# A three-part decoder layer on one core: w2 copied in DRAM and split in place, no weight pieces on GpSimd, sixteen tile buffers, two scatters in flight

## What is computed

```python
shared = _swiglu(flat @ w_in.T) @ w_out.T
g_probs = jax.nn.softmax(flat @ wg.T + gb, axis=-1)          # 2 groups
g_idx = jnp.argmax(g_probs, axis=-1)
e_logits = flat @ we.T + eb                                   # 8 experts, 4 in a group
masked = jnp.where(g_idx[:, None] == egid[None, :], e_logits, -jnp.inf)
p_expert = jax.nn.softmax(masked, axis=-1) * g_prob
topv, topi = jax.lax.top_k(p_expert, TOP_K)                   # TOP_K = 2
h = _swiglu(flat @ w1.T)                                      # 512 wide, the same for all experts
for e in range(NUM_EXPERTS):
    routed = routed + h * w_se[:, e:e + 1] @ w2[e].T
return (shared + routed).reshape(Bs, Ts, C)
```

## Time and profile before

| | us |
|---|---|
| timed runs, median of 3 (lowest, highest) | 945.33 (943.61, 945.38) |
| the profiled execution's own time | 941.11 |
| its span, first to last instruction | 939.3 |
| block 2 begins | about 649 |
| slot numbers known | 725.4 |
| scatters issued, first to last | 726.3 to 773.1 |
| first transposes of the expert loop | 790.4 |
| last PE work of the loop, gathers begin | about 870 to 873 |

### The profile page before, as it was taken

One profiled execution on the slowest core, in us unless ns is written; L12 is line 12 of the kernel. 1 busy time (PEld: TensorE's weight loads), 2 busy tenths in 40 slices (PEclk: granted clock), 3 DMA queues, 4 the chain that ended last, 5 costly groups with the idle time before them and its releaser, 6 DMA issues. The chain is left out here.

```text
span 939.3 us, 17987 instructions
## 1 busy us (share of the span) xinstructions
PE 851.3 (91%) x6115; PEld 741.0 (79%) x6115; DVE 596.2 (63%) x1513; ACT 546.3 (58%) x1667; POOL 304.0 (32%) x318
## 2 busy tenths in 40 slices
PE   8999999999999989999999999998787748999841
PEld 6788888888888878988988898896575637999731
DVE  5787787687778767667767766775768214333153
ACT  4877677677668776866677686775343113554110
POOL 1443124124123434421432341351333750000544
PEclk9999999999999999999999999999897969999976
DMA  7680000000001020000000020010120532664233
GB/s 240 245 312 2 1 0 0 0 0 0 0 1 46 24 68 1 1 23 1 0 22 0 0 80 9 1 46 1 67 68 23 206 152 95 205 199 149 79 90 112
DMA packets 34105, 60.35 MB, mean 64 GB/s; under 512 B 3460, under 2 KB 15108, under 8 KB 34052
## 3 DMA queue, kind: packets, MB, share of 16 engines
q1 hardware_dynamic: 29956, 47.07, 15.0%
q0 software_dynamic: 4096, 12.59, 4.0%
HBM read 33.83 MB, written 25.82 MB: 64 GB/s over the span
## 5 line engine op out<-in xcount | busy, mean ns | idle before, releaser
L420 POOL TENSOR_TENSOR prob<-prob,rsum 128x512 f32<-128x512 f32 x128 | 133.4, 1042 | 395.0 <-DVE rsum L613 395.0
L498 ACT ACTIVATE prob<-psS,nmin 128x128 f32<-128x128 f32 x512 | 181.4, 378 | 6.2 <-DVE nmin L597 3.6
L481 ACT ACTIVATE pT_hi<-psT 128x512 fp32r<-128x512 f32 x128 | 69.6, 595 | 85.6 <-PE psT L752 85.6
L498 ACT ACTIVATION_READ_ACCUMULATOR prob<-psS,nmin 128x1 f32 x512 | 111.9, 218 | 0.0
L582 DVE TENSOR_TENSOR oT_lo<-psT,oT_hi 64x512 fp32r<-64x512 f32 x128 | 88.1, 688 | 23.1 <-ACT oT_hi L486 21.1
L576 DVE TENSOR_TENSOR pT_lo<-psT,pT_hi 128x512 fp32r<-128x512 f32 x128 | 82.3, 685 | 1.6 <-ACT pT_hi L481 1.4
L486 ACT ACTIVATE oT_hi<-psT 64x512 fp32r<-64x512 f32 x128 | 76.1, 594 | 5.6 <-PE psT L143 3.9
L476 ACT ACTIVATE v_hi<-psW 128x512 fp32r<-128x512 f32 x64 | 38.3, 598 | 68.0 <-PE psW L143 68.0
L141 PE MATMUL psT<-pT_lo,v_hi 128*128 128x256 f32 x256 | 73.1, 285 | 4.6 <-DVE pT_lo L576 4.6
L570 DVE TENSOR_TENSOR v_lo<-psW,v_hi 128x512 fp32r<-128x512 f32 x64 | 44.2, 691 | 50.3 <-ACT v_hi L476 50.3
L1022 POOL DMA_INDIRECT stage<-ys,slot x32 | 32.6, 1017 | 128.1 <-DMA ys<-z 99.7
(11 more groups left out here) (252 smaller groups left out, 2501.4 us busy)
## 6 DMA issues: line engine op xcount, KB each, us to landing
hs<-zero SPq DMA_DIRECT2D x1, 9984.0 KB, 31.2
stage<-hs SPq DMA_DIRECT2D x39, 256.0 KB, 2.9
stage<-w SPq DMA_DIRECT2D x10, 512.0 KB, 3.4
ys<-z SPq DMA_DIRECT2D x39, 128.0 KB, 1.9
stage<-ctxT SPq DMA_DIRECT2D x4, 512.0 KB, 4.0
out<-xres SPq DMA_DIRECT2D x16, 128.0 KB
xres<-x SPq DMA_DIRECT2D x3, 512.0 KB, 7.6
stage<-wq SPq DMA_DIRECT2D x2, 512.0 KB, 3.9
```

Source lines behind the costliest of these rows:

```text
L420: nc.gpsimd.tensor_tensor(prob[:, r, :], prob[:, r, :], rsum[:, r].unsqueeze(2).broadcast_to([P, TPG, P]), ALU.mult).then_inc(prob_done, 1)
L481: nc.scalar.activation(pT[0][:, i, :], psT[:, i, :], ACT.Copy).then_inc(pT_hi, 1)
L498: e = nc.scalar.activation(prob[:, n, :], flat(psS[:])[:, n * P:(n + 1) * P], ACT.Exp, bias=nmin[:, n:n + 1], scale=-1.0, accum_out=psums[ ...
```

## The change

- w2 is copied in DRAM, early in block 1, into an internal tensor `w2_raw`. At the start of block 2, SyncE loads it in four DMAs of 1 MB straight into the tensor that later holds the low parts. ScalarE writes the high parts from there (`w2_hi_part`, eight pieces), and VectorE subtracts in place (`w2_lo_part`, eight pieces).
- w_in's parts are made at the end of block 1, the high part on ScalarE, the low part on VectorE, both between the last `pT_split` and the last `oT_split`. GpSimd makes no low part in block 2. The table for Silu is loaded before the last `pT_split`.
- Tiles 12 to 15 of h have slots of their own: `z` for 12 and 13, the routing's scratch tensors `above` and `ties` for 14 and 15 (these wait for `weights_known`).
- Each scatter of tile T for choice c waits until that of tile T-1 for the same choice has landed. The semaphores are per choice now.
- The routing ranks each expert among the 4 of its group instead of among 8, which halves the arrays; `unsel` and `wse` are written once after both rounds (`unselected`). Some units stand in another order to the routing on VectorE.

```diff
+        w2_raw = nc.dram_tensor("w2_raw", [HT, P, NE * D], F32, kind="Internal").ap()
...
-        H_AT = (6, 7, 10, 11, 2, 3, 4, 5, 8, 9, 0, 1)
+        H_AT = (6, 7, 8, 9, 10, 11, 0, 1, 2, 3, 4, 5)
...
+            pieces += [(k_rows(win), wq_hi[:], wq_lo[:], 1.0)]
...
                 sp.dma_start(hs.rearrange("(t p) d -> p t d", p=P),
                              zero[:].unsqueeze(1).broadcast_to([P, NT, HID])).then_inc(slots_zero, 16)
+                sp.dma_start(w2_raw, w2.rearrange("(k p) n -> k p n", p=P)).then_inc(w2_copied, 16)
                 sp.dma_start(craw, ctx_v[:, :, 0:GT]).then_inc(ctx_in, 16)
...
+                act.preload_act_table(ACT.Silu)
                 pT_split(STEPS)
+                act.wait_ge(qk_mm, 2 * STEPS)
+                weights_hi(act, N_ATT + 2, wq_hi[:])
                 oT_split(STEPS, 1)
...
                 pT_split(STEPS)
+                weights_lo(dve, N_ATT + 2, wq_lo[:], wq_hi[:])
                 oT_split(STEPS, 1)
...
+            def h_slot(T):
+
+                if T < HSLOTS:
+                    return chunk(H_AT[T])
+                if T < HSLOTS + 2:
+                    return flat(z[:, 2 * (T - HSLOTS):2 * (T - HSLOTS) + 2, :])
+                return (above, ties)[T - HSLOTS - 2][:]
...
-                for i in range(STAGES, len(late)):
-                    wait_lo(sp, LATE[i - STAGES])
-                    sp.dma_start(piece(N0 + i, late[i][0].shape), late[i][0]).then_inc(stage_in[(N0 + i) % STAGES], 16)
-
-                for n in range(REUSED):
-                    sp.wait_ge(scattered[n], 2 * CHOICES * 16)
-                sp.wait_ge(scattered_rest, (HSLOTS - REUSED) * CHOICES * 16)
+                sp.wait_ge(w2_copied, 16)
+                for k in range(HT):
+                    sp.dma_start(w2s[1][:, k, :].bitcast(F32), w2_raw[k]).then_inc(w2_in[k], 16)
+
+                for c in range(CHOICES):
+                    sp.wait_ge(scattered[c], B * 16)
...
                     for c in range(CHOICES):
+                        if T:
+                            pool.wait_ge(scattered[c], 16 * T)
                         d = nc.gpsimd.indirect_dma_start(
                             hs[:, :], bass.IndirectOffsetOnAxis(ap=slot[:, c, T:T + 1], axis=0), h_slot(T), None,
                             bounds_check=SLOTS - 1, oob_is_err=False)
-                        d.then_inc(scattered[T % HSLOTS] if T % HSLOTS < REUSED else scattered_rest, 16)
+                        d.then_inc(scattered[c], 16)
...
+                def w2_hi_part(i):
+                    k, c = W2_PARTS[i]
+                    act.wait_ge(w2_in[k], 16)
+                    nc.scalar.activation(w2s[0][:, k, c], w2s[1][:, k, c].bitcast(F32), ACT.Copy).then_inc(w2_hi, 1)
...
+                def w2_lo_part(i):
+                    k, c = W2_PARTS[i]
+                    dve.wait_ge(w2_hi, i + 1)
+                    nc.vector.tensor_tensor(w2s[1][:, k, c], w2s[1][:, k, c].bitcast(F32), w2s[0][:, k, c].bitcast(F32),
+                                            ALU.subtract).then_inc(w2_lo, 1)
...
-                for u in range(14, UNITS.index("S10") + 1):
+                for u in range(14, UNITS.index("S10")):
                     unit(u)
+                    w2_lo_part(u - 14)
+                w2_lo_part(6)
+                unit(UNITS.index("S10"))
+                w2_lo_part(7)
```

More of the change, by code:

```diff
@@ L242, in build @@
                    ("xk", "upper"), ("xr", "upper"), ("w1", "lower"), ("w1", "upper"))]
-        PIECES += ["win", "wout"] + [f"w2 {k} {half}" for k in range(HT) for half in ("lower", "upper")]
+        PIECES += ["win", "wout"]
         BY_POOL = ("wk upper", "wr lower", "wr upper", "xv upper", "xr lower", "xk upper", "xr upper",
-                   "w1 lower", "win", "w2 0 lower", "w2 0 upper", "w2 1 lower", "w2 1 upper", "w2 2 lower", "w2 2 upper",
-                   "w2 3 lower")
+                   "w1 lower")
         def wait_lo(eng, name):
@@ L394, in _ @@
                     load(sp, n, pieces[n][0])
-                for i in range(STAGES):
-                    load(sp, len(pieces) + i, late_sources[i])
+                load(sp, len(pieces), late_sources[0])
                 sp.wait_ge(slots_zero, 16)
@@ L928, in build @@
             GSTEPS = 19
[L929 to L934 removed]
+            N0 = PIECES.index("wout")
+            late = [(late_sources[0], wouts[0][:], wouts[1][:])]
+            W2_PARTS = [(k, slice(c * INNER, (c + 1) * INNER)) for k in range(HT) for c in range(2)]
             ROUND = (range(0, 3 * TPG), range(3 * TPG, B))
@@ L1082, in _ @@
                 unit(8)
-                late_hi(4)
-                late_hi(5)
+                bias(3)
                 exps(0)
-                bias(3)
+                w2_hi_part(1)
                 unit(9)
-                late_hi(6)
-                late_hi(7)
+                w2_hi_part(2)
                 exps(1)
                 unit(10)
-                late_hi(8)
-                late_hi(9)
-                for u in range(11, UNITS.index("S10") + 1):
+                w2_hi_part(3)
+                unit(11)
+                w2_hi_part(4)
+                unit(12)
+                w2_hi_part(5)
+                unit(13)
+                w2_hi_part(6)
+                unit(14)
+                w2_hi_part(7)
+                for u in range(15, UNITS.index("S10") + 1):
                     unit(u)
@@ L1164, in gate_ranks @@
                     n = len(ROUND[r])
-                    pe_ = probs[:, tiles, GROUPS:NG]
-                    gsum_, esum_, chosen_, coef_ = (t[:, tiles] for t in (gsum, esum, chosen, coef))
-                    above_, ties_ = above[:, 0:n], ties[:, 0:n]
+                    gsum_, esum_, chosen_, coef_, picked_ = (t[:, tiles] for t in (gsum, esum, chosen, coef, picked))
+                    above_, ties_ = (t[:, 0:n * GROUPS * PER_GROUP * PER_GROUP].rearrange(
+                        "p (t a b) -> p t a b", a=PER_GROUP, b=PER_GROUP) for t in (above, ties))
+                    rank4 = rank[:, tiles].rearrange("p t (g e) -> p (t g) e", g=GROUPS)
                     link, linked = chain(gate_step, r * GSTEPS + 4)
@@ L1312, in _ @@
                 split("S03")
-                unit(8)
                 dve.wait_ge(gate_copied, 3)
@@ L1316, in _ @@
                 gate_maxima(0)
+                unit(8)
                 gate_ranks(0)
@@ L1491, in _ @@
                 pe.wait_ge(experts_known, 1)
[L1492 to L1493 removed]
+                pe.wait_ge(w2_lo, len(W2_PARTS))
                 turn(0)
```

108 lines of the change are left out of this document (41 added, 67 removed).

## The result

The changed kernel takes 917.51 us (median of four runs, 917.14 to 917.67) against 945.36 for the kernel before (four runs, 943.61 to 945.77): a ratio of 0.971, 95% interval 0.969 to 0.973. The forecast was 927.0 with a range of 914 to 938. The time lies in the range; the gain is 27.8 us where 18.3 were forecast. The experiments then showed something that the forecast did not know of: how large the gain is depends on which chip the kernels run, or when. On two chips of the experiments the kernel before takes 917.6 us, and on the one of them where the changed kernel was timed beside it, that takes 913.8.

What follows compares the result with a forecast made beforehand. PE bounds the kernel, except between 650 and 790 us, where it waits; the question is when the expert loop starts. 941.11 profiled, minus 21.0 for the earlier loop, plus 2.7 slow clock: 922.8, or 927.0 as a median; range 914 to 938.

Steps and rivals of the forecast that it cites:

- Block 1's end: End of block 1: the new w_in pair fits DVE's 3.40 us gap but for about 0.2 us, charged as cost.
- Group 1 and 3: Transposes of block 2's groups 1 and 3: shorter PE waits and less slow clock, saving 6.8 and 3.6 us.
- Routing: From H6 to the slot counts: PE, not DVE, sets the counts, 5.7 us after H6 instead of 13.7, saving 8.0.
- A tile's time: Scatters under the new wait: landing 2.86 plus wake-up 0.78, so 3.64 us a tile where it took 2.55.
- PE's readiness at 745: Before the expert loop: PE finishes its own work by about 745 and waits 24 us for the scatters.
- The slow clock at the loop's start: Start of the expert loop: after its wait PE runs at the low clock level, charged 2.7 us.
- What lies behind the loop's start: Loop, gathers and last units, some 149 us: same code on the same data, so only the loop's start matters.
- The offset of 4.2 us to the median: Whole kernel: the profiled execution lies 4.2 us below the median, so 922.8 becomes 927.0 as a median.
- Rival 1: Scatters: the limit doesn't bind, landings come inside 2.55 us and the old pace stays; 910.7 us, chance 10%.
- Rival 2: Scatter stretch: ScalarE held as before, H12's Silu waiting until GpSimd runs out of tiles; 933.9 us, chance 14%.
- Rival 3: Scatter stretch: GpSimd and DVE block each other on eight w2 low parts, at worst 9.8 us; 936.8, chance 7%.
- Rival 4: Scatters: slower than before, longer landings with each tile paying the whole round trip; 956.7 us, chance 6%.

## Why the prediction was right, and where it was not

What is compared here is the profiled execution, 922.8 forecast, 917.14 measured.

- **Block 1's end, 0.2.** Right: the pair fitted the gap. Block 2 began 1.3 us sooner all the same. The windows of 300 to 400 us below, of before and of after (columns as above), show a mean granted clock of 0.98 and of 1.00 with the same code. I take the 1.3 to be mostly that: all 14 profiles fit it. Four have 1.00 in this window, and their first logits copies stand between 647.5 and 648.7 us; ten have 0.98, and theirs stand between 649.0 and 650.2. The changed kernel is in both groups, with 648.28 and, run again, 649.05. So at least 0.8 of the 1.3 us is luck of the execution and not the change.

```profile
300.00:400.00 100.00, 97.06 (x747) 85.21 (x746) 71.72 (x165) 74.89 (x240) 44.36 (x42) 0.98 0.08 27
```

```profile
300.00:400.00 100.00, 97.04 (x765) 85.17 (x762) 73.13 (x168) 75.42 (x242) 45.87 (x43) 1.00 0.08 27
```

- **Group 1 and 3, 6.8 and 3.6.** Right. Up to the transposes of group 3 the forecast was 9.1 sooner and with the 1.3 above 10.4; measured 11.5. The 1.1 more is a wait that I had left before group 1's transposes (657.6 forecast, 655.19 measured, 1.3 of it the earlier start). The slow clock behind that wait was worth its 2.2: PE is 7.0 us sooner at group 1's transposes and 9.1 at group 2's (666.63 against 675.77). Group 1's term was priced apart, by the w_in part put back: 6.7 for the 6.8 forecast.
- **Routing, 8.0.** Right. From group 3's transposes to the slot counts 9.2 us were won; the forecast had 8.0 and 1.3 of clock behind group 3. PE reaches the counts with no wait for DVE, as the walk had it.
- **A tile's time, 3.64.** Right: 3.55 in the steady part, 3.71 on average, and the landing that I read off one place (2.89) is 2.8 to 2.9 in twelve of the other traces (3.16 in one). PE's readiness at 745 (744.46) and its wait of 24 us (23.62) too. The loop was forecast at 769.4 and began at 768.08. That it came so close is in part luck: the slot numbers came 3.1 us before the 707.0 forecast, and the way from there to the loop took 64.2 us instead of 62.4 (15 tiles at 3.71 instead of 3.64 are 1.1 of it; the rest is a first scatter 1.14 us behind the slot numbers instead of 0.8, and 1.64 us between the last two instead of 1.28).
- **The slow clock at the loop's start, +2.7.** Wrong, it was 0. The clock was low, as forecast, but I took its price from a stretch in which PE alone set the time. At the loop's start PE waited in the kernel before as well, for DVE; there I should have asked what it hides behind.
- **What lies behind the loop's start, "the same code on the same data".** Wrong by 1.6 us, the shorter stretch from the gathers on. Neither kernel is free of a hold of DVE there (13.52 and 13.51 us shown as remote in the two traces), so I can't split the 1.6.
- **The offset of 4.2 us to the median.** Wrong by 3.8: by the two profiles of the kernel before it was not an offset but the spread of a hold, which the changed kernel doesn't have. I had carried a difference between two executions of one kernel over to another kernel without asking what it was made of.

Together: 1.3 of the loop's start, 2.7, 1.6 and 3.8 are 9.4 of the 9.5 us. And the forecast, like all its prices, held for a held chip: on a free one the same change brought 3.8 us and not 18.3, and that the comparison fell on a held one was no merit of mine.

**The rivals.** Rival 1 (the limit doesn't bind) has fallen: without the limit the loop starts 15.3 us sooner (753.40 and 768.74, both on free chips). Rival 2 (ScalarE held as before) has fallen for the changed kernel, in whose profiles no Silu is held; a hold did come in the kernels without a limit on held chips, but as one to three shorter ones, of 8 to 11 us the longest, and not as one from H12 until GpSimd ran out of tiles: PE came to the loop at 755 to 763, not 779. One reading of the trace in it needs a word: at 764 us the train of scatters had not stopped for good but paused, between 762.0 and 763.76, for the tile that the held Silu was to make. Rival 3 has fallen, at 2.8 us in place of 9.8 and only visible without the limit. Rival 4, the slower one, fell: the landing was 2.8 us, as the one place had said. But its mechanism, each tile paying the round trip, is what the limit is: 14.9 us. It needs no longer landing to decide, only a chip on which nothing was held before: the limit alone makes the kernel before 14 to 15 us slower there. My chances of 0.90 to 0.07 were built on one chip's trace, and a row marked "remote" was the place to see that.

**A version that beats both.** The changed kernel without the limit takes 898.9 us on a free chip (changed: 913.8, before: 917.6) and 910.6 on a held one (changed: 917.5, before: 945.3). With the limit PE waits 23.6 us for scatters that it need not wait for; without it the hold, where it occurs, falls partly into PE's slack.

## What to carry to other kernels

A bound on transfers in flight makes every transfer pay its landing; price it as landing plus wake-up times their number, and compare with the issuing engine's own pace, which here was 2.55 us a tile against 3.7. A small job on a little-used engine can cost far more than its share when it blocks rows that a full engine waits for: 4.49 us of GpSimd were worth 6.7 us of the kernel. When the profile and the timed runs of one kernel differ by more than the runs among themselves, find the stretch that varies before carrying the difference over, and when a wait names no releaser, try the kernel on another chip before building on it.

## What the hardware showed

- One kernel's time differs between chips: 917.6 us on two, 943.7 to 945.4 in the other comparisons. In the profiles from there ScalarE stands idle for up to 19.78 us beside a train of scatters without a limit, and VectorE goes on about 5 us late beside gathers. Whether it is the chip or the time is open.
- No Silu was held in the six profiles with two scatters in flight, two of them on held chips; with four in flight one was held for 8.11 us.
- SyncE's load stands 2.8 to 2.9 us behind the issue of the last scatter, whether that is one of two in flight or the end of a train.
- A scatter instruction of 0.97 us becomes 1.14 to 1.73 us beside DVE's products and w2 parts, and DVE's parts keep their 1.22 us.
